# Attention by values: where keys are split, when queries are made, and who takes the quotient

## What is computed

```python
q = (jnp.einsum('bld,ed->ble', x, Wq) + bq).reshape(b, l, 16, 8)
kv = (jnp.einsum('bmc,ec->bme', y, Wkv) + bkv).reshape(b, m, 16, 16)
k, v = (kv[..., :8], kv[..., 8:])
att = jax.nn.softmax(jnp.einsum('blhd,bmhd->blmh', q, k) * scale, axis=2)
out = jnp.einsum('blmh,bmhd->blhd', att, v).reshape(b, l, 128)
x = x + jnp.einsum('bld,ed->ble', out, Wo) + bo
```

## Time and profile before

| | us |
|---|---|
| three runs, median (lowest to highest) | 5362.53 (5360.59 to 5368.59) |
| the profiled execution, its own time | 5364.85 |
| its span, first to last instruction | 5363.1 |

### The profile page before, as it was taken

The page is one execution under the profiler, slowest core; times in us unless marked ns, Lnnn a source line. Parts: engine busy times, 40 slices in busy tenths (PEclk is TensorE's granted clock), DMA queues, the critical chain, the costliest instruction groups (busy, mean ns, idle before and its releaser), DMA issues. The chain is left out here.

```text
span 5363.1 us, 99725 instructions
## 1 busy us (share of the span) xinstructions
PE 4418.4 (82%) x34185; PEld 3753.2 (70%) x34185; DVE 3413.8 (64%) x5857; ACT 2278.9 (42%) x4584; POOL 1442.8 (27%) x1142
## 2 busy tenths in 40 slices
PE   5399999975789998998999838777599999987684
PEld 4277777763688888888888836565477777765573
DVE  4477777766655666566556637876677777765545
ACT  0166556552233333333333315554355656653341
POOL 0233333422110101011001006654433334323320
PEclk6599999987789998999999968887799999988887
DMA  7344444420110001000100020000144444420282
GB/s 237 96 92 107 101 93 107 95 49 9 45 27 21 21 17 26 21 21 17 27 20 21 4 63 0 0 0 1 40 102 102 93 108 100 98 54 24 49 181 55
DMA packets 190536, 314.81 MB, mean 59 GB/s; under 512 B 132372, under 2 KB 140870, under 8 KB 190406
## 3 DMA queue, kind: packets, MB, share of 16 engines
q1 hardware_dynamic: 186822, 294.71, 24.5%
q10 hardware_dynamic: 3584, 18.43, 0.9%
HBM read 146.07 MB, written 19.54 MB: 31 GB/s over the span
## 5 line engine op out<-in xcount | busy, mean ns | idle before, releaser
L1232 PE MATMUL a1m_ps_o<-a1m_cn,a1m_prob_t 125*128 125x97 f32 x5376 | 652.9, 279 | 0.2 <-issue 0.2
L1373 ACT ACTIVATE a1m_prob<-a1m_ps_s,a1m_neg_max 128x500 f32<-128x500 f32 x672 | 405.8, 675 | 557.1 <-DVE a1m_neg_max L1311 557.1
L1232 PEld LDWEIGHTS a1m_ps_o<-a1m_cn,a1m_prob_t 125*128 125x128 f32 x5376 | 640.8, 198 | 0.4 <-issue 0.4
L1308 DVE TENSOR_REDUCE a1m_bank_max<-a1m_ps_s 128x1 f32<-128x500 f32 x672 | 455.4, 678 | 145.6 <-PE a1m_ps_s L1198 144.1
L1162 POOL TENSOR_TENSOR a1m_cxt<-a1m_raw,g_zeros 98x1500 fp32r<-98x1500 f32 x32 | 86.7, 2711 | 1428.5 <-PE a1m_ps_s L1198 1384.9
L1198 PE MATMUL a1m_ps_s<-a1m_cxt,a1m_qhi 98*128 98x500 f32 x1344 | 436.1, 406 | 6.7 <-DVE a1m_qlo L1300 5.0
L818 ACT ACTIVATE a0m_prob_t<-a0m_ring 125x448 f32<-125x448 f32 x768 | 384.2, 546 | 106.0 <-PE a0m_ring L525 104.5
L818 ACT ACTIVATE a2m_prob_t<-a2m_ring 125x448 f32<-125x448 f32 x768 | 384.2, 547 | 105.2 <-PE a2m_ring L525 103.6
L725 DVE TENSOR_REDUCE a2m_bank_max<-a2m_ps_s 112x1 f32<-112x1000 f32 x256 | 302.5, 1182 | 157.4 <-PE a2m_ps_s L574 157.4
L725 DVE TENSOR_REDUCE a0m_bank_max<-a0m_ps_s 112x1 f32<-112x1000 f32 x256 | 302.5, 1182 | 153.9 <-PE a0m_ps_s L574 153.9
L1214 PE MATMUL a1m_ps_t<-g_ident,a1m_prob 128*125 128x128 f32 x2688 | 373.2, 275 | 1.1 <-ACT a1m_prob L1373 0.8
(11 more groups left out here) (787 smaller groups left out, 9926.3 us busy)
## 6 DMA issues: line engine op xcount, KB each, us to landing
a0m_ks<-a0m_k_hi SPq DMA_DIRECT2D x256, 187.5 KB
a2m_ks<-a2m_k_hi SPq DMA_DIRECT2D x256, 187.5 KB
a0m_ks<-a0m_k_lo SPq DMA_DIRECT2D x128, 187.5 KB
a2m_ks<-a2m_k_lo SPq DMA_DIRECT2D x128, 187.5 KB
ctx_t<-cprep_tr ACTq DMA_DIRECT2D x32, 562.5 KB
a0m_raw<-ctx_t SPq DMA_DIRECT2D x32, 562.5 KB
a1m_raw<-ctx_t SPq DMA_DIRECT2D x32, 562.5 KB
a2m_raw<-ctx_t SPq DMA_DIRECT2D x32, 562.5 KB
```

What stands on the lines that cost most here:

```text
L1232: m = pe.matmul(ps_o[at, 0:CO], prob_t[:, u % 2, t, at], cn[:, h, t, :], start=(t == 0), stop=(t == KT - 1))
L1308: dve.tensor_reduce(bank_max[:, s, k:k + 1], ps_s[:, k, 0:BK], AX.X, ALU.max).then_inc(bank_maxed, 1)
L1373: act.activation(prob[:, s, k * BK:(k + 1) * BK], ps_s[:, k, 0:BK], ACT.Exp, bias=neg_max[:, s:s + 1]).then_inc(exped, 1)
```

## The change

- k_full and `k_copied` go. ScalarE writes the rounded key bank straight to k_hi (`high_keys`), and its wait for the earlier key DMAs comes with it. VectorE makes k_lo as the PSUM bank minus k_hi (`low_keys`), after the maxima of unit 0 (banks 0 and 1) and of unit 1 (bank 2).
- T3, T4 and T6 of a key half wait for `k_kept`, which VectorE's subtraction now gives.
- `asks(i, h)`: queries of the next pair are made in h0, not in h1 (in the ramp still in h = 1).
- GpSimd takes the queries' low part (`low_queries`) and the quotient (`quotient`); in its half the pick comes first. VectorE keeps bias and rounding of the queries and the sum over heads.

```diff
-            def split_keys(i, h, c):
...
-                pool.wait_ge(k_copied, BANKS * n + c + 1)
...
+            def low_queries(i, h):
...
+                pool.wait_ge(q_rounded, i + 2)
+                if h == 0 and up(4 * i):
+                    pool.wait_ge(own_made, 4 * i)
+                low = slice(2 * qd, 3 * qd)
+                pool.tensor_tensor(qp[low, :], qf[low, :], qp[low, :].bitcast(F32), ALU.subtract).then_inc(q_split, 1)
+
+            def quotient(i, h):
...
+                m, p = 4 * i + h - 1, (h - 1) % 4
+                pool.wait_ge(reduced, m + 1)
+                pool.wait_ge(inverted, m + 1)
+                if asks(i, h):
+                    pool.wait_ge(q_split, i + 2)
+                if p == 0 and up(i):
+                    pool.wait_ge(projected, i)
+                pool.tensor_tensor(av[:, groups * (p % 2):groups * (p % 2 + 1), p // 2, :],
+                                   av_sum[:].rearrange("p (x l) -> p x l", x=groups),
+                                   rec[:].rearrange("p (x l) -> p x l", x=groups), ALU.mult).then_inc(av_made, 1)
...
                 m = 4 * i + h
+                if among(m + 3, halves) and not (isinstance(m, int) and m == -3):
+                    pick_queries(m + 3, i if h == 0 else i + 1, (h + 3) // 2 % 2, (h + 3) % 2, 12 * m)
                 if among(m - 1, halves):
                     own_rows(m - 1, (h - 1) % 2)
-                if h % 2 and among(2 * i + h // 2 + 2, total):
-                    for c in range(BANKS):
-                        split_keys(i, h, c)
-                if among(m + 3, halves):
+                if asks(i, h):
+                    low_queries(i, h)
...
+                if among(m - 1, halves):
+                    quotient(i, h)
...
                     else:
-                        pe.wait_ge(k_copied, BANKS * (n + 2) + c + 1)
+                        pe.wait_ge(k_kept, BANKS * (n + 2) + c + 1)
...
-                if h == 1 and among(i + 1, NP):
+                if asks(i, h):
                     queries(i)
...
+            def low_keys(i, h, c):
...
+                n = 2 * i + h // 2 + 2
+                if c == 0 and up(n):
+                    for x in range(quads):
+                        dve.wait_ge(keys_in[x], 16 * parts * n)
+                dve.wait_ge(high_made, BANKS * n + c + 1)
+                at = slice(c * BK, (c + 1) * BK)
+                dve.tensor_tensor(k_lo[:, at], ring[where["X", c] % 3][:, 0:BK], k_hi[:, at].bitcast(F32), ALU.subtract
+                                  ).then_inc(k_kept, 1)
...
                 unit(0)
-                if h == 1 and among(i + 1, NP):
+                if x_live:
+                    low_keys(i, h, 0)
+                if asks(i, h):
                     queries(i)
+                if x_live:
+                    low_keys(i, h, 1)
                 if live:
                     invert(m - 1)
                 unit(1)
+                if x_live:
+                    low_keys(i, h, 2)
                 if live:
-                    outputs(i, h)
+                    sum_heads(m - 1)
...
+            def high_keys(i, h, c):
...
+                if c == 0 and up(n):
+                    for x in range(quads):
+                        act.wait_ge(keys_in[x], 16 * parts * n)
                 act.wait_ge(k_made, BANKS * n + c + 1)
-                if up(n):
-                    act.wait_ge(k_kept, BANKS * (n - 1) + c + 1)
-                act.activation(k_full[:, c * BK:(c + 1) * BK], ring[where["X", c] % 3][:, 0:BK], ACT.Copy
-                               ).then_inc(k_copied, 1)
+                act.activation(k_hi[:, c * BK:(c + 1) * BK], ring[where["X", c] % 3][:, 0:BK], ACT.Copy
+                               ).then_inc(high_made, 1)
```

More of the change, by code:

```diff
@@ L341, in attend_turned @@
         raw = st.sb("raw", [CO, 2, S])
-        k_full = st.sb("k_full", [P, S])
         k_hi, k_lo = st.sb("k_hi", [P, S], F32R), st.sb("k_lo", [P, S], F32R)
@@ L360, in attend_turned @@
         keys_in = [st.sem(f"keys_in{n}") for n in range(quads)]
-        (prepared, filled, k_made, k_copied, high_made, k_kept, v_made, v_kept, q_made, q_biased, q_rounded, q_split,
+        (prepared, filled, k_made, high_made, k_kept, v_made, v_kept, q_made, q_biased, q_rounded, q_split,
          picked, scored, maxed, combined, max_high, max_split, shift_made, shifted, turned, exped, summed, o_kept,
          den_made, inverted, own_made, reduced, av_made, projected, out_kept) = (st.sem(x) for x in (
-             "prepared", "filled", "k_made", "k_copied", "high_made", "k_kept", "v_made", "v_kept", "q_made", "q_biased",
+             "prepared", "filled", "k_made", "high_made", "k_kept", "v_made", "v_kept", "q_made", "q_biased",
              "q_rounded", "q_split", "picked", "scored", "maxed", "combined", "max_high", "max_split", "shift_made",
@@ L376, in among, with asks @@
             return not isinstance(v, int) or 0 <= v < n
+        def asks(i, h):
+            return h == (1 if isinstance(i, int) and i < 0 else 0) and among(i + 1, NP)
         def pairs(eng, half):
@@ L449, in own_rows @@
                     ALU.mult).then_inc(own_made, 1)
-            def split_keys(i, h, c):
-                n = 2 * i + h // 2 + 2
-                at = slice(c * BK, (c + 1) * BK)
-                pool.wait_ge(k_copied, BANKS * n + c + 1)
[L456 to L463, removed]
+            def low_queries(i, h):
[15 more added lines that the diff above has]
+                                   rec[:].rearrange("p (x l) -> p x l", x=groups), ALU.mult).then_inc(av_made, 1)
             def pick_queries(w, j, b, hf, done):
@@ L480, in half @@
                 m = 4 * i + h
+                if among(m + 3, halves) and not (isinstance(m, int) and m == -3):
+                    pick_queries(m + 3, i if h == 0 else i + 1, (h + 3) // 2 % 2, (h + 3) % 2, 12 * m)
                 if among(m - 1, halves):
                     own_rows(m - 1, (h - 1) % 2)
-                if h % 2 and among(2 * i + h // 2 + 2, total):
-                    for c in range(BANKS):
-                        split_keys(i, h, c)
-                if among(m + 3, halves):
+                if asks(i, h):
+                    low_queries(i, h)
+                if isinstance(m, int) and m == -3:
                     pick_queries(m + 3, i if h == 0 else i + 1, (h + 3) // 2 % 2, (h + 3) % 2, 12 * m)
+                if among(m - 1, halves):
+                    quotient(i, h)
             pool.memset(vals[:, :, :, :, 25:qd], 0.0).then_inc(filled, 1)
@@ L505, in turned_scores @@
                     if isinstance(m, int) and m == 0:
-                        pe.wait_ge(k_copied, 2 * BANKS)
+                        pe.wait_ge(k_kept, 2 * BANKS)
                         pe.wait_ge(prepared, dve_sets)
@@ L546, in values @@
                     if m == -2:
-                        pe.wait_ge(k_copied, c + 1)
+                        pe.wait_ge(k_kept, c + 1)
                     elif c == 0:
-                        pe.wait_ge(k_copied, 2 * BANKS)
+                        pe.wait_ge(k_kept, 2 * BANKS)
                     else:
@@ L597, in denominators @@
                 pe.wait_ge(o_kept, m + 1)
-                if h == 1 and among(i + 1, NP):
+                if asks(i, h):
                     pe.wait_ge(q_biased, i + 2)
-                elif h == 1:
+                elif h == 1 and up(i):
                     pe.wait_ge(out_kept, i)
@@ L617, in shifts @@
                 if isinstance(w, int) and w < 2:
-                    pe.wait_ge(*((q_biased, 1) if w == 0 else (shifted, 1)))
+                    pe.wait_ge(q_biased, w + 1)
+                    if w == 1:
+                        pe.wait_ge(shifted, 1)
                 else:
@@ L628, in queries @@
                 j = i + 1
-                if up(i):
-                    pe.wait_ge(out_kept, i)
                 if up(j):
-                    pe.wait_ge(shifted, 4 * i + 2)
+                    pe.wait_ge(shifted, 4 * i + 1)
                 for x in range(quads):
@@ L708, in queries @@
                 dve.wait_ge(q_made, j + 1)
+                if up(j):
+                    dve.wait_ge(q_split, j)
                 dve.tensor_tensor(qf[:].rearrange("p (x c) -> p x c", x=quads),
@@ L716, in queries @@
                 dve.tensor_copy(qp[:], qf[:]).then_inc(q_rounded, 1)
-                dve.wait_ge(q_rounded, j + 1)
-                low = slice(2 * qd, rows)
-                dve.tensor_tensor(qp[low, :], qf[low, :], qp[low, :].bitcast(F32), ALU.subtract).then_inc(q_split, 1)
+            def low_keys(i, h, c):
[7 more added lines that the diff above has]
+                                  ).then_inc(k_kept, 1)
             def maxima(i, h, u):
@@ L748, in invert, with sum_heads @@
                 dve.reciprocal(rec[:], ps_m[:, 0:gw]).then_inc(inverted, 1)
-            def outputs(i, h):
-                m, p = 4 * i + h - 1, (h - 1) % 4
+            def sum_heads(m):
                 dve.wait_ge(own_made, m + 1)
```

(16 more changed lines are left out.)

## The result

| | before | after |
|---|---|---|
| median (lowest to highest), us | 5365.56 (5360.59 to 5372.6) | 5310.06 (5307.06 to 5312.16) |
| profiled execution; its span, us | 5364.85; 5363.1 | 5307.06; 5305.3 |

A forecast was written before the change was run, and what follows sets the result against it. TensorE's own order was taken to set the time. Steady pairs +5.4, clock -35.9 and ramps -14.4 us net -45, from 5364.85 to 5320, that is 5318 beside the median; range 5278 to 5366.

The forecast's parts named there:

- low_keys 0.68: VectorE's new key subtraction of 500 columns out of PSUM takes 0.68 us, six times per pair.
- T3 later by 0.60, T6 by 0.74: In h1 and h3 TensorE's T3 and T6 wait for VectorE's subtraction: 0.60 and another 0.74, sum 1.34 us.
- A key half of 14.31: h3, and h1 likewise, last 12.97 + 1.34 = 14.31 us.
- h0 of 14.89: h0 loses 1.64 us of slow clock and gains 0.70 of queries: 15.83 becomes 14.89 us.
- The wait goes, with 1.6 to spare: Keys land 12.7 us behind h3's unit 0, TensorE needs them after 14.31: the DMA wait before h0 goes.
- The clock stays at 2.4 GHz: No idle stretch as long as 1.35 us ahead of h0, so no slow clock: 19.7 + 16.2 = 35.9 us back.
- The ramp, 4.3 and 2.9 per attention: In each attention's ramp the first key wait shrinks by 4.3 us, the second by 2.9; two attentions 14.4.
- GpSimd's new work and the pick beside everything: GpSimd's low part, quotient (bounds 0.33 and 1.56 us) and earlier pick delay nothing; VectorE's row shifts lose up to 0.7.
- The clock as before: Rival, 14%: new waits in h3 or a remaining DMA wait leave TensorE at 1.2 GHz as often: 5354 us.
- the late DMA: Rival, 5%: the key DMA lands 1.6 us later than counted, so wait and slow clock before h0 stay: 5395.
- Shorter waits: Rival, 12%: T6 finds its ring bank free, 60 x 0.74 = 44 us less: 5274.
- The slower one: Rival, 14%: VectorE's subtraction on TensorE's path costs 1.25 us, giving 5386, or the clock falls every key half, giving 5416.

The follow-up runs named there:

- the experiment with the low part twice: Changed kernel with each VectorE subtraction of low_keys done once more before, into a spare tile: 5390.86 us, ratio 1.0052.
- the experiment with T3 and T6 behind: Changed kernel with, in h1 and h3, the denominators put before T3 and unit 2 before T6: 5246.59 us, ratio 0.978.
- the experiment with the tenth turned score: Changed kernel with SyncE sending the keys of h3 only after the tenth of twelve turned scores of h3: 5345.8 us, ratio 0.9969.
- the last experiment: Changed kernel with the queries' low part and the quotient back on VectorE: 5313.85 us, ratio 0.9906.
- the queries in h0 alone: Kernel before the change with only the queries moved from h1 to h0: 5391.79 us, ratio 1.0054.
- round 1's run: Changed kernel with SyncE sending the keys of h3 only after round 1 of h3: 5455.54 us, ratio 1.0166.
- the eleventh's: Changed kernel with SyncE sending the keys of h3 only after the eleventh of twelve turned scores of h3: 5461.91 us, ratio 1.0178.

## Why the prediction held, step by step

The direction, the mechanism and the size held (5318 in 5278 to 5366, measured 5310). The terms:

- **low_keys 0.68.** Right: the least, median and most of line 741, with those of the lines moved to GpSimd, the quotient and the queries' low part:

```profile
L741 DVE TENSOR_TENSOR a0m_k_lo<-a0m_ring,a0m_k_hi x96: 665/669/680, 219.3 to 1088.6; 128x500 fp32r<-128x500 f32 x96
L471 POOL TENSOR_TENSOR a0m_av<-a0m_av_sum,a0m_rec x64: 540/545/551, 274.7 to 1140.1; 128x168 f32<-128x168 f32 x64
L460 POOL TENSOR_TENSOR a0m_qp<-a0m_qf,a0m_qp x16: 1126/1137/1139, 221.1 to 1042.9; 32x448 fp32r<-32x448 f32 x16
L761 DVE CAST a0m_shift<-a0m_neg_max x64: 170/171/907, 238.5 to 1120.0; 112x4 fp32r<-112x4 f32 x64
```

 Line 709, with the same kinds of operands, was the right row to take it from the earlier trace rows. It never grows beyond 680 ns. In the changed kernel only 4 of the 192 subtractions of both attentions run beside a GpSimd instruction; with the queries back in h1 34 do, and they take 665 to 680 as well. *By the Trainium skill (SBUF — State Buffer, the section on the two separate sides) VectorE contends with GpSimd for the shared port pair only in a 2-port perf mode or with two SBUF inputs; the trace agrees for this subtraction, whose first input is in PSUM.*
- **T3 later by 0.60, T6 by 0.74.** Right: unit 0 to unit 1 takes 4.23 against 3.62 before, unit 1 to unit 2 4.11 against 3.38: 0.61 and 0.73. Both waits are real and in series (the experiment with the low part twice), and both can be filled (the experiment with T3 and T6 behind).
- **A key half of 14.31.** Mis-sized: 14.17 to 14.18. The base of 12.97 was h2's length. h2 is no key half: its own stretch from unit 0 to unit 1 is 3.70. A key half without waits, put together from its own rows of before, is 3.63 + 3.38 + 2.72 + 3.12 = 12.85. The 0.13, 60 times, is 8 us of the saving that the forecast missed. Between the profiled executions it missed 13 (45 against 57.8): these 8, 4 since a pair of before without the slow clock was 56.35 and 56.52 and not 56.30, 2 of the ramp and 3.5 outside the attentions, less 2 for the queries (next) and 3 for the last halves, which the sum didn't have.
- **h0 of 14.89.** 14.96. The queries cost 0.77 there, not 0.70; 28 times, 2 us the other way.
- **The wait goes, with 1.6 to spare.** Right in its numbers: h3's first key DMA goes out 8.01 behind unit 0, and SyncE's row stands here:

```profile
638.89 0.51 SPq L414 DMA_DIRECT2D a0m_ks<-a0m_k_hi  x1
```

 With the 4.67 of before it lands at 643.56, 1.5 ahead of unit 0 at 645.06. In the experiment with the tenth turned score the same DMA goes out 2.4 later, and unit 0 waits 0.86: the edge is 1.5 us away.
- **The clock stays at 2.4 GHz.** Right in all steady pairs. The reason given, that no idle stretch as long as 1.35 is left ahead of h0, was good enough here and is too simple as a rule: in the experiment with the tenth turned score waits of 1.0 were enough in three pairs.
- **The ramp, 4.3 and 2.9 per attention.** 4.6 and 2.0 in attention 0, 4.4 and 3.7 in attention 2, and 0.8 to 0.9 of clock behind, which the sum left out: 16.5 in all against 14.4. The timeline of TensorE in attention 0's ramp, to be read beside the earlier trace rows:

```profile
227.03 1.56 PE L587 MATMUL a0m_ps_s<-a0m_ks,a0m_qs 96*112 96x500 f32 x3 [8.58 <-DMA a0m_ks<-a0m_k_hi]
...
250.51 1.56 PE L587 MATMUL a0m_ps_s<-a0m_ks,a0m_qs 96*112 96x500 f32 x3 [2.02 <-DMA a0m_ks<-a0m_k_hi]
```

- **GpSimd's new work and the pick beside everything.** Right. The quotient takes 0.545, within the bounds of 0.33 and 1.56, the low part 1.137. But the 1.54 to 1.56 of line 719 was no price of the instruction: before, GpSimd was at work beside it each time, and the same instruction back on VectorE, in the last experiment, takes 0.62:

```profile
L730 DVE TENSOR_TENSOR a0m_qp<-a0m_qf,a0m_qp x16: 617/617/618, 221.8 to 1044.3; 32x448 fp32r<-32x448 f32 x16
```

 The term was in VectorE's load alone, not in the sum, so the forecast didn't suffer. The feared meeting happens, in 13 of the 64 halves of attention 0: the row shift (line 761 of the changed kernel) takes up to 907 ns instead of 171, and nobody waits for it.
- **The rivals.** The clock as before and the late DMA: excluded by the rows of h0. Shorter waits: excluded, 0.73 against 0.74. The slower one: its mechanism is there and its price was not; with 0.67 more per subtraction the run came out at 5391, where 5386 had been worked out for 0.57 more.

One thing the prediction did not weigh: it took the order of T3, T6, denominators and unit 2 as given. Four fifths of the two waits it counted so closely could be had back by changing that order (1.06 of 1.34).

## What to carry to other kernels

Read an engine that works through a fixed order by the distances between the starts of one recurring instruction, and take the base of a half from rows of the same kind of half. When a step moves to an engine on whose result that order waits, its duration counts in series each time, unless work that needs nothing from it is queued ahead of the waiting instruction: here that reordering was worth 64 us, more than the change itself. And when a wait goes, look at what it did to TensorE's clock behind it: here the wait itself only changed its name, and most of the gain was the clock.

## What the runs showed of the hardware

- In the kernel before, waits for a DMA of 1.35 to 1.5 us at unit 0 of h0 were followed by 1.2 GHz in 12 of 13 pairs of attention 0 and in 6 of 12 of attention 2; so were one of 1.78 and one of 2.36, and not those of 1.26, 1.29 and 1.69. With the queries in h0 alone, only 21 of 60 waits, most of 1.35 to 1.5 us, were followed by it.
- In the tenth's run, waits of 0.67 to 0.91 were followed by it in none of 15 pairs, waits of 1.00 to 1.26 in 3 of 13, one of 1.89 and not one of 1.59. In round 1's run (1.59 to 2.32) it followed in 28 of 30, for an excess of 3.0 to 3.3 us in 23 and of 1.6 in five; in the eleventh's (2.6 to 3.2) in all, with an excess of only 1.6 to 2.7.
- Waits for VectorE inside a key half, one of 0.9 and one of 1.2 to 1.3 us with the low part twice, were followed by no fall. So the length of a wait alone does not tell. What else does (what TensorE did before, or when the wait falls) stays open.
- GpSimd took 0.545 us for 128 x 168 from two tiles where VectorE took 0.33 undisturbed, and 1.14 for 32 x 448 where VectorE took 0.62 undisturbed. Beside GpSimd VectorE took up to 1.07 for the first and 1.56 for the second.
